# Last image's row-class-0 sums and last column pairs moved from GpSimd to VectorE, and image 0's second normalisation issued four gaps later

## The chip, the cores and the metric

The kernel runs on one core of a Trainium2 chip. The metric is the device time of one execution in microseconds (us), smaller is better. The engines are TensorE (PE, with PEld for its weight loads), VectorE (DVE), ScalarE (ACT), GpSimd (POOL) and SyncE (SP), which issues nearly all DMAs.

## The reference

For two images of 32 channels and 48x48 pixels the kernel computes a cross-scale attention block and then a two-dimensional cosine transform:

```python
x = x + _L0_conv_ref(_gn(x), W1, b1, a1, W2, b2, a2, Wa, ba, aa, Wd, bd)
x = x + _L1_conv_ref(_gn(x))
# _L0_conv_ref, the part that matters here, one image at a time
yi = jnp.einsum('blc,bqc->blq', wn, xp)          # 576 keys x 2304 queries
yi = jax.nn.softmax(yi * SOFTMAX_SCALE, axis=1)  # over the keys
yt = jax.vmap(tconv)(yi, raw_w)                  # stride-2 transposed conv, 6x6 patches
yd = lax.conv_general_dilated(yt, Wd, (2, 2), ((1, 1), (1, 1)), ...)
return (yd + bd) / 6.0
# _L1_conv_ref: y = Dh @ x @ Dw.T per channel, Dh and Dw cosine matrices
```

`_gn` is a group normalisation with one channel per group. The second one (on `x1`, the result of the first line) is the "normalisation" of the title.

## The kernel before, in words

**Queries, keys and classes.** An image's 2304 queries lie in six row classes of 384 (`NCH` = 6), each class in three column tiles of 128 (`TPC` = 3). So there are 12 chunks (`NG`), numbered k = 0 to 11, image 0 being k = 0 to 5, and 36 softmax tiles (`NT`). Each softmax tile is a slot of `nt`, 128 queries by 24x24 keys kept with a zero column (25 per row).

**Attention as sums.** The two convolutions after the softmax are turned into sums of shifted tiles. GpSimd first adds tiles of neighbouring row classes (`total`, lines 667 to 673, called by `row_sums` and, for the classes z5 and z0 that wrap around the image's edge, by `wrapped_sums`). It then adds column tiles in pairs (`pair(k, which)`, lines 647 to 661, two adds per chunk). After that PE transposes and adds (`turn(k, blk)`, line 866, five blocks of keys per chunk, six transposes into one PSUM bank), DVE or ACT copies the bank to `yf` (`sums_copied`, line 1346 on DVE for blocks 0, 2 and 4, line 1084 on ACT for blocks 1 and 3), and PE multiplies with the turned filters (`values(k, blk)`, line 882, five accumulating matmuls per chunk). DVE adds the result to the image (`finish`, line 1361).

**Step numbers.** Everything is issued in an order written out by hand: a loop over 47 steps s on each engine. Chunk k is turned in the steps 11 + 3k to 13 + 3k (j = 0, 1, 2 inside the chunk), so k = 8 has s = 35 to 37, k = 9 has s = 38 to 40, k = 10 has s = 41 to 43 and k = 11 has s = 44 to 46. Each engine executes its instructions in this order, so an instruction that waits holds all that is written behind it. The last three chunks ("flush", `NG - LAG` on) use an order in which a block is copied shortly before its `values`.

**Side jobs.** Work beside the main loop is placed in gaps, three per step. The table `SPREAD` gives each job its first gap and its pace; DVE's and ACT's part comes one or two gaps behind PE's by `BEHIND_PE`. The jobs that matter here belong to the second half of image 0: `x1n` (three DVE instructions, line 1390, `xd` from `v2`, first gap 109 = step 36, gap 1), `zn` (16 transposes of 32 columns three times on PE, line 892, copied out by ACT, line 1094), `d1` (eight cosine matmuls twice, line 902) and `d2` (three long matmuls twice, line 913). `x1n` needs the inverse root of the variance that GpSimd computes in `deviation` (line 614), which stands behind six row sums and three pairs in GpSimd's own order.

**Waits inside turn.** Block m = 5k + blk of `turn` waits until an earlier bank is copied: `wait_copied(m - 2)` up to m = 48 (`FLUSH` is 46), `wait_copied(m - 4)` from 49 on. For m = 47, the block (k = 9, blk = 2), this is the DVE copy of (9, 0). Block 0 of a chunk also waits for the two column pairs of its chunk (`s_pair`).

Of the kernel before, what the change touches and what calls it, by code (L numbers as in the profile page):

```python
# [8 lines left out]
ALU = mybir.AluOpType  # L9
# [3 lines left out]
B, C, H, W = 2, 32, 48, 48  # L13
CR = C // 2
Q = H * W
HL, WL = H // 2, W // 2
# [13 lines left out]
TPC = 3  # L30
JW = W // TPC
NT = B * NCH * TPC
NG = B * NCH
# [7 lines left out]
KP = WL + 1  # L41
PT = (HL + 2) * KP + 2
KROWS = 5
KB = 5
# [3 lines left out]
TURNED = ["z1", "z2", "z3", "z4", "z5", "z0"]  # L48

P0, P1, P2, P3, P4, P5, PAIR0 = 0, 3, 6, 9, 12, 15, (18, 21)  # L50
DOWN0, UP5 = 24, 27
COLS = 30
# [45 lines left out]
    ("norm", 1, 1, 25, 1), ("inorm", 1, 2, 43, 3), ("keys", 1, 2, 46, 3),  # L98
    ("wst", 1, 1, 50, 1), ("bias_a", 1, 1, 53, 1), ("residual", 0, 1, 33, 1),
    ("emb", 1, 2, 57, 3), ("ek", 1, 2, 80, 2), ("residual", 1, 1, 66, 1),  # L100
    ("stats", 0, 6, 98, 1), ("deviation", 0, 1, 105, 1), ("x1n", 0, 3, 109, 2), ("zn", 0, 3, 115, 1),
    ("d1", 0, 2, 122, 2), ("d2", 0, 2, 128, 2)]
CLASSES = [2, 3, 4, 5, 0, 1]


# [28 lines left out]
def sums_done(b, name, jb):  # L134

    return NSUMS * b + SUMS[name] + SUMS_EVERY[name] * jb + 1


def program(nc, x, params, dct, x1_copy, out):
# [16 lines left out]
    with ExitStack() as ctx:  # L156
# [6 lines left out]
        def sem(name):  # L163
            return ctx.enter_context(nc.semaphore(name))

        def sems(name, n=B):
            return [sem(f"{name}{i}") for i in range(n)]
# [31 lines left out]
        nt = sb("nt", [128, NTILES, PT])  # L199
# [35 lines left out]
        zn = sb("zn", [W, C, H])  # L235
# [50 lines left out]
        s_up5 = sems("row_before_shifted_in", TPC)  # L286
# [22 lines left out]
        s_add = sem("row_sums")  # L309
        s_zt = sem("sums_turned")  # L310
        s_pair = sem("columns_paired")
        s_ya = sem("sums_copied_act")
        s_yd = sem("sums_copied_dve")
        s_mb = sem("taps_block_done")
# [54 lines left out]
        def perform(jobs, handlers):  # L369

            for name, b, i in jobs:
                if name in handlers:
                    handlers[name](b, i)
# [44 lines left out]
        def place_of(k):  # L418

            b, i = k // NCH, k % NCH  # L420
            return ((P0, 0), (P1, -1), (P2, -1), (P3, -1), (P4, -1), (PAIR0[b], 0))[i]

        def wait_copied(eng, m):

# [141 lines left out]
        def _(pool):  # L566
# [13 lines left out]
            for blk, row in ((0, 0), (BLOCKS - 1, ROWS - 1)):  # L580
                at = match_rows_at(1, blk, row)
                link(pool.memset(F(strided(mimg[:, :], at, (TILE, TPC), (1, JW))), 0.0))
            link(pool.memset(F(strided(mimg[32:64, :], match_rows_at(0, 0, 0), (BLOCK, BLOCKS), (JW, ROWS))), 0.0))
            at = match_rows_at(TPC + 1, 0, 0) + JW - 1
# [62 lines left out]
            def pair(k, which):  # L647

                if k >= 2:
                    pool.wait_ge(s_zt, KB * (k - 1))  # L650
                place, dr = place_of(k)
                at = (dr + 1) * KP + 1
                dst = nt[:, COLS + 2 * (k % 2) + which, :]
                if which == 0:
                    ins = pool.tensor_tensor(dst[:, at - 1:at + KP * HL], nt[:, place, at - 1:at + KP * HL],  # L655
                                             nt[:, place + 1, at:at + KP * HL + 1], ALU.add)
                else:
                    ins = pool.tensor_tensor(dst[:, at:at + KP * HL], nt[:, place + 2, at:at + KP * HL],  # L658
                                             nt[:, place + 1, at - 1:at + KP * HL - 1], ALU.add)
                ins.then_inc(s_pair, 1)  # L660
                pool.wait_ge(s_pair, 2 * k + which + 1)

            def odd_taps(b, _):
# [4 lines left out]
            def total(b, name, jb, dst, to, one, row1, other, row2, rows):  # L668

                n = KP * rows - 1  # L670
                pool.tensor_tensor(nt[:, dst, (to + 1) * KP + 1:(to + 1) * KP + 1 + n],  # L671
                                   nt[:, one, (row1 + 1) * KP + 1:(row1 + 1) * KP + 1 + n],
                                   nt[:, other, (row2 + 1) * KP + 1:(row2 + 1) * KP + 1 + n],
                                   ALU.add).then_inc(s_add, 1)
                pool.wait_ge(s_add, sums_done(b, name, jb))
                if name in TURNED and jb:
                    pair(NCH * b + TURNED.index(name), jb - 1)

            def wrapped_sums(b, jb):

                for n in (2 * jb, 2 * jb + 1):
                    name, at = ("z5", "z0")[n // TPC], n % TPC
                    if name == "z5":
                        total(b, "z5", at, P4 + at, -1, P4 + at, -1, DOWN0 + at, 1, HL)
                    else:
                        pool.wait_ge(s_up5[at], 16 * (b + 1))
                        total(b, "z0", at, PAIR0[b] + at, 0, PAIR0[b] + at, 0, UP5 + at, -1, HL)
# [46 lines left out]
        def _(pe):  # L734
# [114 lines left out]
            def turn(k, blk):  # L849

                b = k // NCH
                n, r = KEYS[blk], KROWS * blk
                m = KB * k + blk
                if blk == 0:
                    pe.wait_ge(s_pair, 2 * (k + 1))
                if m >= FLUSH + 3:
                    wait_copied(pe, m - 4)
                elif m >= 2:
                    wait_copied(pe, m - 2)
                if m < 2 or FLUSH < m < FLUSH + 3:  # L860
                    pe.wait_ge(s_ex, FILL if m < 2 else NT)
                place, dr = place_of(k)
                first, second = COLS + 2 * (k % 2), COLS + 2 * (k % 2) + 1
                work = ((first, 0, 0), (first, 1, -1), (second, 2, 0), (place + 2, 1, 1), (place + 2, 3, -1), (place, -1, 1))
                for at, (tile, column, shift) in enumerate(work):
                    last = nc.tensor.matmul(turned(sums_bank(m), n, column), keys_at(tile, r + dr, n, shift),  # L866
                                            ident[:, :], start=at == 0, stop=at == len(work) - 1, is_transpose=True,
                                            skip_group_check=True)
                last.then_inc(s_zt, 1)
# [52 lines left out]
            for s in range(steps):  # L922
                k, j = divmod(s - BEGIN, TPC)
# [213 lines left out]
        def _(dve):  # L1137
# [200 lines left out]
            def sums_copied(k, blk):  # L1338
# [5 lines left out]
                else:  # L1344
                    dve.wait_ge(s_mf, misc_no["norm", B - 1, 0] + 1)
                nc.vector.tensor_copy(strided(yf[0:n, blk, :], 0, (1, TPC), (W, ROWS), (TPC, JW)),  # L1346
                                      planes(sums_bank(m), n)).then_inc(s_yd, 1)

            def finish(k, si):

                b, t = k // NCH, ZT[k % NCH]
                if si == 0:
                    dve.wait_ge(s_mb, KB * (k + 1))
                    if k % NCH == 0:
                        dve.wait_ge(s_xres[b], 1)
                        dve.wait_ge(s_apart[b], 1)
                rows = ROWS - 1 if si and t == NCH - 1 else ROWS
                both = v2[2 * C * b:2 * C * (b + 1), :]
                image = strided(both, W * (t + si), (W * NCH, rows), (1, W))
                tap = strided(yt[2 * C * si:2 * C * (si + 1), k % 2, :], 0, (W, rows), (1, W))  # L1360
                nc.vector.scalar_tensor_tensor(out=image, in0=tap, scalar=1.0 / 6.0, in1=image, op0=ALU.mult,  # L1361
                                               op1=ALU.add).then_inc(s_fin, 1)
                dve.wait_ge(s_fin, 2 * k + si + 1)

            def join_taps(b, part):

                first, n = ((2, 4), (0, 2))[part]
                dims = (W * NCH, ROWS), (W, n), (1, W - 1)
                even = strided(x1(b), W * first + 1, *dims)
                odd = strided(v2[2 * C * b + C:2 * C * (b + 1), :], W * first, *dims)  # L1370
                nc.vector.tensor_tensor(even, even, odd, ALU.add).then_inc(s_x1[b], 1)  # L1371
                dve.wait_ge(s_x1[b], part + 1)
# [55 lines left out]
            for s in range(steps):  # L1428
                k, j = divmod(s - BEGIN, TPC)
                if s + 1 == FILL:  # L1430
                    inverse_sum(s)
                if s + 1 < NT:
                    maximum(s + 1)
                if s + 1 < FILL:
                    inverse_sum(s)
                perform(gaps["dve"].get((s, 0), []), handlers)
                if k >= 1 and j == 1:
                    finish(k - 1, 0)
                if k >= 1 and j == 2:
                    finish(k - 1, 1)  # L1440
                if FILL <= s + 1 < NT:
                    inverse_sum(s + 1)
                if k >= 0 and j == 0:
                    sums_copied(k, 0)
                perform(gaps["dve"].get((s, 1), []), handlers)
                if k >= 0 and j == 1:
                    sums_copied(k, 2)
                if k >= 0 and j == 2:
                    sums_copied(k, 4)
                    if k and (k - 1) % NCH >= NCH - 2:  # L1450
                        join_taps((k - 1) // NCH, (k - 1) % NCH - (NCH - 2))
                perform(gaps["dve"].get((s, 2), []), handlers)
            perform(behind[:4], handlers)
            finish(NG - 1, 0)
# [37 lines left out]
```

## Time and profile before

| | us |
|---|---|
| median of 3 runs | 246.06 |
| lowest and highest | 244.96, 249.21 |
| the profiled execution, device time | 246.48 |
| its span, first to last instruction | 244.1 |

| engine | busy us | share of the span |
|---|---|---|
| PE | 178.3 | 73% |
| DVE | 144.3 | 59% |
| POOL | 132.2 | 54% |
| ACT | 116.6 | 48% |

The profiled execution lies 0.42 us above the median. Its device time is 2.4 us more than its span; what lies around the span is the same for both kernels. The mean granted clock of PE is 0.869 of full speed. In the profile a block `turn` is a row "PE L866 ... x6", a block `values` a row "PE L882 ... x2" (each product is recorded as two matmuls).

### The profile page before, as it was taken

Reading aid. Unit: us, or ns where it says so; the run is one execution under the profiler, and the core shown is the slowest. Engines: PE = TensorE matmul, PEld = TensorE weight load, DVE = VectorE, ACT = ScalarE, POOL = GpSimd, SP = SyncE. Lnnn points to the kernel's source line nnn. Section 1 sums busy time; section 2 is a strip of 40 time slices with the busy share of each in tenths; the row PEclk is TensorE's granted clock in tenths of the full one; section 3 lists DMA queues with packets and bytes.
Section 4 is the critical chain, followed back from the end, with each engine's and each line's share of the span. In section 5 each row is a group of like instructions: output and inputs, shape, how many; then the busy total and the mean of one; then the engine's idle time right before and its main releaser. Section 6 shows DMA issues by size and latency. Waiting matters only on the chain. (4 is left out here: it accounts for less than half of the span.)

```text
span 244.1 us, 3460 instructions
## 1 busy us (share of the span) xinstructions
PE 178.3 (73%) x1088; PEld 143.9 (59%) x1088; DVE 144.3 (59%) x291; ACT 116.6 (48%) x211; POOL 132.2 (54%) x114
## 2 busy tenths in 40 slices
PE   0586508576673799751999999969986799992484
PEld 0424507574453577641888878857874587870482
DVE  5678825354224766999465545575793733649502
ACT  4876322575736796632365876536552040220110
POOL 8273001033758999496419499999989586000000
PEclk9996556979795899996799999999999799999555
DMA  5350266551260000244633214400261000000522
GB/s 147 76 96 2 45 123 103 132 125 45 45 103 6 3 0 0 42 82 80 172 99 84 56 32 73 81 8 0 60 137 48 0 4 0 3 0 0 112 37 48
DMA packets 16872, 14.09 MB, mean 58 GB/s; under 512 B 9974, under 2 KB 14646, under 8 KB 16726
## 3 DMA queue, kind: packets, MB, share of 16 engines
q1 hardware_dynamic: 15974, 12.98, 26.5%
q10 hardware_dynamic: 880, 0.89, 1.2%
q8 instruction: 9, 0.15, 0.2%
q14 instruction: 9, 0.07, 0.1%
HBM read 2.14 MB, written 1.18 MB: 14 GB/s over the span
## 5 line engine op out<-in xcount | busy, mean ns | idle before, releaser
L671 POOL TENSOR_TENSOR nt<-nt 128x599 f32<-128x599 f32 (+1 forms) x54 | 73.4, 1360 | 32.6 <-ACT nt L1074 23.5
L882 PE MATMUL yt<-yf,kf 125*128 125x384 f32 (+1 forms) x120 | 50.3, 504 | 6.1 <-DVE yf L1346 4.2
L866 PEld LDWEIGHTS zt<-ident,nt 128*125 128x125 f32 (+1 forms) x312 | 41.6, 180 | 12.9 <-issue 3.5
L866 PE MATMUL zt<-ident,nt 128*125 128x128 f32 (+1 forms) x312 | 43.9, 278 | 0.0
L1066 ACT ACTIVATE nt<-ps,negm 128x576 f32<-128x576 f32 x31 | 22.9, 739 | 39.6 <-DVE negm L1329 39.5
L845 PE MATMUL ps<-wh,vh 128*128 128x288 f32 x62 | 17.8, 371 | 26.9 <-DVE wr L1325 17.0
L1074 ACT ACTIVATE nt<-nt,rps 128x599 f32<-128x599 f32 x36 | 28.6, 796 | 15.4 <-DVE rps L1336 15.2
L1329 DVE TENSOR_REDUCE negm<-ps 128x1 f32<-128x576 f32 x31 | 23.3, 753 | 15.8 <-PE ps L845 15.5
L845 PEld LDWEIGHTS ps<-wh,vh 128*128 128x128 f32 x62 | 10.3, 206 | 32.2 <-DVE wr L1325 17.7
L655 POOL TENSOR_TENSOR nt<-nt 128x601 f32<-128x601 f32 x12 | 16.5, 1371 | 15.3 <-PE zt L866 14.7
L882 PEld LDWEIGHTS yt<-yf,kf 125*128 125x128 f32 (+1 forms) x120 | 19.4, 197 | 8.3 <-DVE yf L1346 4.6
L1346 DVE COPY yf<-zt 125x384 f32<-125x384 f32 (+1 forms) x31 | 21.4, 692 | 4.6 <-issue 4.1
L1084 ACT ACTIVATE yf<-zt 125x384 f32<-125x384 f32 x21 | 14.3, 681 | 10.4 <-PE zt L866 10.4
L658 POOL TENSOR_TENSOR nt<-nt 128x600 f32<-128x600 f32 x12 | 17.7, 1477 | 0.9
L1276 DVE TENSOR_TENSOR mimg<-mst,mhi 96x288 fp32r<-96x288 f32 x16 | 10.6, 664 | 10.7 <-DMA vl<-mimg 5.4
L1336 DVE RECIPROCAL rps<-psm 128x1 f32<-128x1 f32 x36 | 5.8, 160 | 14.8 <-ACT nt L1066 14.6
L1361 DVE SCALAR_TENSOR_TENSOR v<-yt,v 64x384 f32<-64x384 f32 (+1 forms) x24 | 13.2, 548 | 1.8 <-PE yt L882 1.3
L845 PE MATMUL ps<-wl,vh 128*128 128x288 f32 x62 | 14.2, 313 | 0.0
L845 PE MATMUL ps<-wh,vl 128*128 128x288 f32 x62 | 14.2, 313 | 0.0
L845 PE MATMUL ps<-wr,vr 128*128 128x288 f32 x62 | 14.0, 309 | 0.0
L1094 ACT ACTIVATE zn<-pm 48x512 f32<-48x512 f32 x6 | 3.4, 588 | 21.9 <-PE pm L892 21.9
L614 POOL TENSOR_TENSOR mv<-mv,mhalf 32x1 f32<-32x1 f32 x2 | 1.1, 540 | 21.9 <-DVE mv L1149 21.8
(160 smaller groups left out, 319.3 us busy)
## 6 DMA issues: line engine op xcount, KB each, us to landing
nt<-nt SPq DMA_DIRECT2D x12, 285.2 KB, 3.5
vh<-mimg SPq DMA_DIRECT2D x24, 72.0 KB, 2.6
vl<-mimg SPq DMA_DIRECT2D x24, 72.0 KB, 2.5
emb<-emq SPq DMA_DIRECT2D x32, 18.8 KB, 1.8
v<-x SPq DMA_DIRECT2D x2, 288.0 KB, 4.0
vh<-mimg SPq DMA_DIRECT2D x12, 48.0 KB, 2.2
vl<-mimg SPq DMA_DIRECT2D x12, 48.0 KB, 2.2
x_copy<-v SPq DMA_DIRECT2D x2, 288.0 KB, 2.8
```

The costliest lines, as they stand in the source:

```text
L655: ins = pool.tensor_tensor(dst[:, at - 1:at + KP * HL], nt[:, place, at - 1:at + KP * HL], nt[:, place + 1, at:at + KP * HL + 1], ALU.add)
L658: ins = pool.tensor_tensor(dst[:, at:at + KP * HL], nt[:, place + 2, at:at + KP * HL], nt[:, place + 1, at - 1:at + KP * HL - 1], ALU.add)
L671: pool.tensor_tensor(nt[:, dst, (to + 1) * KP + 1:(to + 1) * KP + 1 + n], nt[:, one, (row1 + 1) * KP + 1:(row1 + 1) * KP + 1 + n], nt[:, o ...
L845: last = nc.tensor.matmul(scores_of(t)[:, h, 0:HALF], queries(m, i, jb), w[b][:, HALF * h:HALF * (h + 1)], start=n == 0, stop=n == 3)
L866: last = nc.tensor.matmul(turned(sums_bank(m), n, column), keys_at(tile, r + dr, n, shift), ident[:, :], start=at == 0, stop=at == len(wor ...
L882: nc.tensor.matmul(yt[:, k % 2, 0:CHUNK], kf[b][0:n, blk, :], yf[0:n, blk, :], start=blk == 0, stop=blk == KB - 1).then_inc(s_mb, 1)
L1066: nc.scalar.activation(strided(nt[:, tile_of(g, jb), :], KP + 1, (KP * HL // 2, 2), (KP, HL // 2), (1, WL)), strided(scores_of(t)[:, 0, :] ...
L1074: nc.scalar.activation(tile, tile, ACT.Copy, scale=rps[:, k:k + 1]).then_inc(s_pn, 1)
L1084: nc.scalar.activation(strided(yf[0:n, blk, :], 0, (1, TPC), (W, ROWS), (TPC, JW)), planes(sums_bank(m), n), ACT.Copy).then_inc(s_ya, 1)
L1329: nc.vector.tensor_reduce(negm[:, t % 2:t % 2 + 1], scores_of(t)[:, :, 0:HALF], AX.XY, ALU.max, negate=True).then_inc(s_mx, 1)
L1346: nc.vector.tensor_copy(strided(yf[0:n, blk, :], 0, (1, TPC), (W, ROWS), (TPC, JW)), planes(sums_bank(m), n)).then_inc(s_yd, 1)
L1361: nc.vector.scalar_tensor_tensor(out=image, in0=tap, scalar=1.0 / 6.0, in1=image, op0=ALU.mult, op1=ALU.add).then_inc(s_fin, 1)
```

## The change

The three sums of row class 0 of the last image (`z0`, b = 1) and the two column pairs of the chunks 10 and 11 are issued by DVE instead of GpSimd. The sums come behind the copy of (8, 4), in step 37; the pairs of chunk 10 behind the copy of (9, 4), in step 40; those of chunk 11 behind the copy of (10, 4), in step 43. PE's `turn(10, 0)` and `turn(11, 0)` wait for DVE's pairs. In `SPREAD` the jobs `x1n`, `zn`, `d1` and `d2` of image 0 start four gaps later.

```diff
-    ("stats", 0, 6, 98, 1), ("deviation", 0, 1, 105, 1), ("x1n", 0, 3, 109, 2), ("zn", 0, 3, 115, 1),
-    ("d1", 0, 2, 122, 2), ("d2", 0, 2, 128, 2)]
+    ("stats", 0, 6, 98, 1), ("deviation", 0, 1, 105, 1), ("x1n", 0, 3, 113, 2), ("zn", 0, 3, 119, 1),
+    ("d1", 0, 2, 126, 2), ("d2", 0, 2, 132, 2)]
...
+        def add_pair(eng, k, which):
+            place, dr = place_of(k)
+            at = (dr + 1) * KP + 1
+            dst = nt[:, COLS + 2 * (k % 2) + which, :]
+            if which == 0:
+                return eng.tensor_tensor(dst[:, at - 1:at + KP * HL], nt[:, place, at - 1:at + KP * HL],
+                                         nt[:, place + 1, at:at + KP * HL + 1], ALU.add)
+            return eng.tensor_tensor(dst[:, at:at + KP * HL], nt[:, place + 2, at:at + KP * HL],
+                                     nt[:, place + 1, at - 1:at + KP * HL - 1], ALU.add)
...
-                if name in TURNED and jb:
+                if name in TURNED and jb and (b < B - 1 or name != "z5"):
                     pair(NCH * b + TURNED.index(name), jb - 1)
...
                     name, at = ("z5", "z0")[n // TPC], n % TPC
+                    if b == B - 1 and name == "z0":
+                        continue
...
                 if blk == 0:
-                    pe.wait_ge(s_pair, 2 * (k + 1))
+                    if k < NG - 2:
+                        pe.wait_ge(s_pair, 2 * (k + 1))
+                    else:
+                        pe.wait_ge(s_other, 2 * (k - NG + 3))
...
+            def last_sums():
+                b, g = B - 1, NG - 1
+                for at in range(TPC):
+                    if at == 0:
+                        dve.wait_ge(s_add, sums_done(b, "z4", TPC - 1))
+                    dve.wait_ge(s_up5[at], 16 * B)
+                    n = KP * HL - 1
+                    dst = nt[:, PAIR0[b] + at, KP + 1:KP + 1 + n]
+                    nc.vector.tensor_tensor(dst, dst, nt[:, UP5 + at, 1:1 + n], ALU.add).then_inc(s_last, 1)
+
+            def last_pair(k):
+                dve.wait_ge(s_zt, KB * (k - 1))
+                if k == NG - 2:
+                    dve.wait_ge(s_add, sums_done(B - 1, "z5", TPC - 1))
+                else:
+                    dve.wait_ge(s_last, TPC)
+                for which in range(2):
+                    add_pair(nc.vector, k, which).then_inc(s_other, 1)
...
                     if k and (k - 1) % NCH >= NCH - 2:
                         join_taps((k - 1) // NCH, (k - 1) % NCH - (NCH - 2))
+                if k == NG - 4 and j == 2:
+                    last_sums()
+                if k >= NG - 3 and j == 2 and k < NG - 1:
+                    last_pair(k + 1)
                 perform(gaps["dve"].get((s, 2), []), handlers)
```

**DVE's order from step 35 to step 39.** Before; COPY yf is a bank's copy, SCALAR_TENSOR_TENSOR v is `finish`, TENSOR_SCALAR xd is `x1n`:

```order
L1346 COPY yf<-zt 125x3x128
L1361 SCALAR_TENSOR_TENSOR v<-yt,v 64x8x48
L1390 TENSOR_SCALAR xd<-v,mv 32x768
L1346 COPY yf<-zt 125x3x128
L1390 TENSOR_SCALAR xd<-v,mv 32x768
L1361 SCALAR_TENSOR_TENSOR v<-yt,v 64x8x48
L1346 COPY yf<-zt 100x3x128
L1390 TENSOR_SCALAR xd<-v,mv 32x768
L1346 COPY yf<-zt 125x3x128
```

And in the changed kernel, where TENSOR_TENSOR nt are the three sums:

```order
L1355 COPY yf<-zt 125x3x128
L1391 SCALAR_TENSOR_TENSOR v<-yt,v 64x8x48
L1355 COPY yf<-zt 125x3x128
L1391 SCALAR_TENSOR_TENSOR v<-yt,v 64x8x48
L1355 COPY yf<-zt 100x3x128
L1367 TENSOR_TENSOR nt<-nt 128x599 x3
L1420 TENSOR_SCALAR xd<-v,mv 32x768
L1355 COPY yf<-zt 125x3x128
L1420 TENSOR_SCALAR xd<-v,mv 32x768 x2
```

The copies in these rows are those of the blocks (8, 0), (8, 2), (8, 4) and (9, 0). `x1n` no longer stands ahead of the copies of (8, 2) and (8, 4); three sums and one `x1n` now stand ahead of the copy of (9, 0).

**DVE's order around the pairs of chunk 10**, from the copy of (9, 4), the changed kernel:

```order
L1355 COPY yf<-zt 100x3x128
L431 TENSOR_TENSOR nt<-nt 128x601
L433 TENSOR_TENSOR nt<-nt 128x600
L1355 COPY yf<-ps 125x3x128
L1391 SCALAR_TENSOR_TENSOR v<-yt,v 64x8x48
```

The two adds stand between the copies of (9, 4) and (10, 0), where nothing stood before; the same pair of rows stands between the copies of (10, 4) and (11, 0).

**PE's order from `turn(9, 4)` to `turn(10, 1)`.** Before, with one half of `d1` (L902) in it:

```order
L866 MATMUL zt<-ident,nt 100x8x16 x6
L902 MATMUL pm<-cosm,zn 96x48 x8
L882 MATMUL yt<-yf,kf 128x384
L866 MATMUL ps<-ident,nt 125x8x16 x6
L882 MATMUL yt<-yf,kf 128x384
L866 MATMUL ps<-ident,nt 125x8x16 x6
```

In the changed kernel:

```order
L875 MATMUL zt<-ident,nt 100x8x16 x6
L891 MATMUL yt<-yf,kf 128x384
L875 MATMUL ps<-ident,nt 125x8x16 x6
L891 MATMUL yt<-yf,kf 128x384
L875 MATMUL ps<-ident,nt 125x8x16 x6
```

Only `values(9, 2)` is left between `turn(9, 4)` and `turn(10, 0)`. Both halves of `d1` now come after `turn(10, 2)`; between `turn(10, 4)` and `turn(11, 0)` stand `values(10, 2)` and one half of `d2`, and the other half of `d2` stands behind `turn(11, 2)`.

## Rows read from the trace of the kernel before

**Rows 1.** The page, part 1: engine, busy us (share), instructions.

```profile
PE 178.3 (73%) x1088; PEld 143.9 (59%) x1088; DVE 144.3 (59%) x291; ACT 116.6 (48%) x211; POOL 132.2 (54%) x114
```

**Rows 2.** The chain that ended last: start, us, what.

```profile
190.50 1.65 PE yt L882 x2
...
210.17 1.05 PE pm L913 x6
...
219.14 0.67 DVE yf L1346
```

**Rows 3.** The waits from 183 to 222 us: total, times, longest.

```profile
PE yt L882 <- DVE yf L1346: 4.2, 2, 3.5
...
DVE xd L1390 <- POOL mv L614: 3.9, 1, 3.9
```

**Rows 4.** The timeline of DVE: start, us, what, [idle before <- releaser].

```profile
188.22 1.64 DVE L1390 TENSOR_SCALAR xd<-v,mv 32x768 f32<-32x768 f32 x1 [3.86 <-POOL mv L614]
189.78 0.66 DVE L1346 COPY yf<-zt 125x384 f32<-125x384 f32 x1
```

**Rows 5.** Busy time by stage; behind the engines PE's granted clock, DMA.

```profile
187.00:190.50 3.50, 0.04 (x2) 0.01 (x1) 2.29 (x3) 0.68 (x1) 3.26 (x4) 1.00 0.00 0
190.50:194.00 3.50, 3.50 (x10) 2.44 (x11) 1.91 (x3) 0.00 (x0) 0.89 (x2) 0.52 0.00 0
194.00:221.00 27.00, 26.99 (x210) 20.90 (x208) 13.73 (x22) 6.61 (x11) 10.77 (x8) 1.00 0.01 2
```

**Rows 6.** The timeline of PE: turn (8,3), (10,0), (11,0), (11,2).

```profile
186.22 0.82 PE L866 MATMUL zt<-ident,nt 128*125 128x128 f32 x6
...
203.76 0.82 PE L866 MATMUL ps<-ident,nt 128*125 128x128 f32 x6
...
213.01 0.82 PE L866 MATMUL ps<-ident,nt 128*125 128x128 f32 x6
...
215.62 0.82 PE L866 MATMUL zt<-ident,nt 128*125 128x128 f32 x6
```

**Rows 7.** DVE's copy of (11,2), behind the last row above.

```profile
216.53 0.67 DVE L1346 COPY yf<-zt 125x384 f32<-125x384 f32 x1 [0.16 <-PE zt L866]
```

**Rows 8.** The timeline of POOL: sums of z5; second pair of chunk 10.

```profile
188.20 2.76 POOL L671 TENSOR_TENSOR nt<-nt 128x599 f32<-128x599 f32 x2
...
196.41 1.45 POOL L658 TENSOR_TENSOR nt<-nt 128x600 f32<-128x600 f32 x1
```

**Rows 9.** The timeline of DVE while POOL is idle.

```profile
219.85 1.72 DVE L1371 TENSOR_TENSOR v<-v 32x1504 f32<-32x1504 f32 x1
...
225.13 0.94 DVE L1371 TENSOR_TENSOR v<-v 32x752 f32<-32x752 f32 x1
...
228.48 1.85 DVE L1390 TENSOR_SCALAR xd<-v,mv 32x768 f32<-32x768 f32 x3 [0.72 <-POOL mv L614]
```

**Rows 10.** DVE adds of 288 columns: POOL idle, then POOL busy.

```profile
34.71 0.46 DVE L1323 TENSOR_TENSOR wl<-wim,wh 128x288 fp32r<-128x288 f32 x1 [4.76 <-ACT wr L1057]
...
104.17 1.28 DVE L1323 TENSOR_TENSOR wl<-wim,wh 128x288 fp32r<-128x288 f32 x1
105.49 1.42 DVE L1324 TENSOR_TENSOR wr<-wim,wr 32x288 fp32r<-32x288 f32 x1
```

**Rows 11.** POOL adds of 624 columns: DVE idle, then beside Rows 10.

```profile
51.41 1.29 POOL L671 TENSOR_TENSOR nt<-nt 128x624 f32<-128x624 f32 x1 [12.56 <-ACT nt L1074]
...
102.30 5.91 POOL L671 TENSOR_TENSOR nt<-nt 128x624 f32<-128x624 f32 x4 [3.28 <-ACT nt L1074]
```

**Rows 12.** Stages of PE alone: us, PE busy, granted clock, DMA.

```profile
107.40:111.00 3.60, 0.00 (x0) 1.00 0.67 107
111.00:114.70 3.70, 0.00 (x0) 0.63 0.38 65
...
118.00:119.00 1.00, 1.00 (x4) 0.60 0.16 43
```

**Rows 13.** The page, part 5: ACT's copies of zn.

```profile
L1094 ACT ACTIVATE zn<-pm 48x512 f32<-48x512 f32 x6 | 3.4, 588 | 21.9 <-PE pm L892 21.9
```

More of the change, by code:

```diff
@@ L311, in program @@
         s_pair = sem("columns_paired")
+        s_last = sem("last_row_sums")
+        s_other = sem("last_columns_paired")
         s_ya = sem("sums_copied_act")
@@ L650, in pair @@
                     pool.wait_ge(s_zt, KB * (k - 1))
[L651 to L660, printed above, removed]
+                add_pair(nc.gpsimd, k, which).then_inc(s_pair, 1)
                 pool.wait_ge(s_pair, 2 * k + which + 1)
```

## The prediction, made before the changed kernel ran

> **What bounds the kernel now.** I read the page first: PE is busy 73% of the span, DVE 59%, GpSimd 54% [rows 1]. No engine is full, so I followed the chain that ended last. It runs on PE alone from 190.50 us, block after block, until DVE's copy of the last turned block at 219.14 [rows 2]; the rest of the span, 25 us, is a chain on DVE, then PE, that both kernels share. So the change is worth what it does to the moment at which `turn(11, 4)` is done.
>
> Then I read the waits. In this stretch PE has one long wait, 3.46 us before `values(8, 2)`, for a DVE copy, and DVE has one of 3.86 us, before the first `x1n`, for GpSimd's inverse root [rows 3, 4]. They are one wait. `x1n` stands ahead of the copy of (8, 2); DVE can start it at 188.22, GpSimd's next add holds it for about 1 us, and the copy follows at 189.78. PE's granted clock, which was 1.00 during the wait, is 0.52 from 190.5 to 194, that is the lower level, 1.2 GHz instead of 2.4, for nearly all of it [rows 5]. In those 3.5 us PE did the work of 1.8, so the clock cost another 1.7. Together the stall is worth 3.5 + 1.7 = 5.2 us. Behind it PE is busy 26.99 of 27.00 us at full clock [rows 5]: there every new wait of PE adds its full length.
>
> **Edit 1, `x1n` and what follows it four gaps later.** It removes the 5.2 us: the copy of (8, 2) then waits for its turned block only. `zn`, `d1` and `d2` are the same instructions as before. No DMA moves: SP's order is unchanged, and ACT only gets its copies later. But moving PE's side jobs takes away cover, which I price below. The three groups of transposes of `zn` now stand together. The third needs the bank that ACT empties after the first, and ACT has the copy of (9, 3), 0.68, ahead of its own 0.59 [rows 13]: 0.2 + 0.7 + 0.6 = 1.5 us against 1.2 of PE's work on two groups. **Wait added: 0.3 us.**
>
> **Edit 2, seven adds leave GpSimd.** GpSimd had the pairs of chunk 10 ready at 197.9 and PE took them at 203.76 [rows 6, 8]; those of chunk 11 were as early against 213.01. GpSimd is 6 us ahead, so taking 7 x 1.4 us from it gains nothing. The Trainium skill (GPSIMD Engine Reference, Engine selection) would have a two-input elementwise add on VectorE, with GpSimd about half as fast, which speaks for the move; the rows say that the adds are shorter but not that anyone waits for them. What it would be if someone did is the last case below.
>
> **Edit 3, the same seven adds on DVE.** DVE has no add of 600 columns in this trace. Its nearest ones, with GpSimd idle, are 1504 columns in 1.72 us and 752 in 0.94 [rows 9], so 1.04 ns per column and 0.16 fixed: 0.78 us for 600. The upper end for one is GpSimd's own time, 1.45 [rows 8]. What matters is where they stand.
>
> *The three sums* stand ahead of the copy of (9, 0), and `turn(9, 2)` waits for that copy. Without the old stall PE is through `turn(8, 3)` at 186.9. A block takes 0.65 us, so six more blocks (`values(8, 2)` to `turn(9, 1)`) bring it to **190.8**. DVE copies (8, 4) when `turn(8, 4)` is done, 188.2 + 0.2 (the delay that [rows 6, 7] show, 216.28 to 216.53) + 0.68, so it is free at 189.1. With GpSimd idle the three sums would end at 191.4, `x1n` (1.85 / 3 = 0.62 [rows 9]) at 192.0, the copy at 192.7. But GpSimd is not idle: it does the sums of z5 from 188.20 on [rows 8], now three in a row to about 192.3 by themselves.
>
> What happens when both add shows at 104 us. DVE's add of 288 columns, 0.46 alone, took 1.28 and 1.42 while GpSimd ran back to back [rows 10], and GpSimd's four took 5.91 with their gaps instead of 4 x 1.29 + 0.2 = 5.4 [rows 11]. That looks like taking turns: each DVE add waits for the end of GpSimd's add, then GpSimd waits for DVE's.
>
> Taking turns: GpSimd's first sum ends at 189.5, DVE's first streams 0.6 to 190.1, GpSimd's second 1.25 to 191.4, DVE's second to 192.0, GpSimd's third to 193.3, DVE's third to 194.0. Then `x1n` 194.6, copy of (9, 0) 195.3. **PE waits from 190.8 to 195.3, 4.5 us.** The bounds are 1.9 us (no interference; 192.7) and this 4.5. I take the upper one, since the rows nearest to it, at 104 us, show a turn of GpSimd before every DVE add.
>
> *The pairs of chunk 10* stand behind the copy of (9, 4). After `turn(9, 4)` DVE needs 0.2 + 0.68 + 2 x 0.78 = 2.45 us, GpSimd being idle by then. PE has `values(9, 2)`, 0.65, before `turn(10, 0)`: the half of `d1` that stood there, 1.5 us, has moved away. **Wait added: 1.8 us.**
>
> *The pairs of chunk 11* likewise: 2.45 us, covered by `values(10, 2)`, 0.65, and half of `d2`, 1.05 / 2 = 0.5 [rows 2]. **Wait added: 1.3 us.**
>
> Behind DVE's adds its later instructions slip too (copies, `finish`), but PE waits for the pairs first, so they are in these numbers. The tail is unchanged: DVE's copy of (11, 4) still follows `turn(11, 4)`.
>
> **The sum.** New waits 4.5 + 0.3 + 1.8 + 1.3 = 7.9 us; removed 3.5 of wait and 1.7 of slow clock. That is +2.7 if PE's clock stays at full speed, and +4.4 if the new 4.5 us wait costs the 1.7 again. Against the profiled execution's 246.48 these are **249.2** and **250.9**. It lies 0.4 above the median of 246.06, less than the runs scatter (244.96 to 249.21), so I don't correct for it. Does the clock fall? The old wait of 3.46 us ended just as it fell; in the long idle time from 107.4 it was still 1.00 up to 111.0 and averaged 0.63 over the next 3.7 us, so it fell after about 4.6 us [rows 5, 12]. A wait of 4.5 lies between: nearly even, slightly for staying.
>
> **The cases.** 2% of 246.06 is 4.9 us, about what a measurement of this kernel can tell from no change: faster is below 241.1, slower above 251.0.
>
> - *Turns, clock stays*: 249.2. Chance 0.33. Forecast.
> - *Turns, clock falls*: 250.9. Chance 0.25, of which a third lies above 251.0.
> - *DVE keeps its turn.* The three sums have no wait between them once the first has run, while at 104 us each DVE instruction waited for the one before. If DVE's second and third add come before GpSimd gets back, the sums end at 191.5, but `x1n` meets GpSimd's second sum and ends at 193.2, copy at 193.9. PE's wait is 3.2 instead of 4.5: 247.9. Chance 0.20.
> - *No interference.* The wait is 1.9: new waits 5.3 against 5.2 removed: 246.6. Against it stand the 1.28 and 1.42. Chance 0.10.
> - *The clock stays low for longer.* After the idle time at 107.4 PE ran at half speed from 114.7 to about 118.8, and the clock had been low since about 112, some 6.8 us in all [rows 12], twice as long as at 190.5. If the clock falls in PE's wait at 195 and PE works 6.9 us at half speed instead of 3.5, that costs 1.7 more: 252.6, slower by 2.7%. It decides from a wait in which the clock falls and that is followed by a further wait, and the 1.8 us wait at `turn(10, 0)` comes soon after. For it: PE's next blocks are broken by that wait. Against it: dense blocks ended the low clock after 3.5 us at 190.5. Chance 0.07.
> - *The shorter adds count.* If PE's pace in the last chunks hangs on the seven adds, each is 1.4 - 0.8 = 0.6 us shorter on DVE, 4.2 us in all: 246.48 - 4.2 = 242.3, and lower if the 5.2 us go as well. This is the Trainium skill's preference taken at its word. The 6 us by which the pairs are early speak against it. Chance 0.05, half of it over 2% faster.
>
> So the likeliest is 249.2, slower by 1.3% but within 2%. Slower than 251.0: 0.07 + a third of 0.25, 0.15. Faster: 0.03. Within: 0.82. The range 246.0 to 251.3 leaves out the last two cases and the edges of two others, about 0.2.
>
> **What the profile after would show.** The 3.86 us wait of DVE for the root is gone and PE runs without a gap to about 190.8. Then PE waits before `turn(9, 2)` for DVE's copy of (9, 0), 4.5 us if the engines take turns (DVE's sums 1.1 to 1.9 us each, GpSimd's second and third sum 1.9 instead of 1.25), 3.2 if DVE's come in a row, 1.9 if there is no interference (0.78 each). Two waits for DVE's pairs, 1.8 and 1.3 us, precede `turn(10, 0)` and `turn(11, 0)`. DVE's copy of (11, 4) starts at 221.9 with a full clock (219.14 before). The prediction is wrong if the sums find GpSimd done, if DVE's adds of 600 columns take much more or less than 0.8, or if the clock behaves otherwise.

## The result and the profile after

The changed kernel takes **253.75 us** (median of 4 runs, 252.78 to 255.46) against 245.51 (median of 4, 244.75 to 249.21): ratio 1.035, 95% interval 1.028 to 1.043. It is slower by 8.2 us. The prediction said 249.2, slower by 1.3% and within 2%, with a range up to 251.3. The direction was right, the size was not. The ratios and intervals here and below leave out executions over 1.5% slower than the fastest of their kernel, which the medians include, and three executions that profiles were taken of (e1, e2, e4) are among those left out, since PE's clock was lower in them ahead of the part that is compared.

I compare the two profiled executions (255.46 and 246.48 us) by one **stretch**: from the start of `values(7, 4)`, the last PE block before the changed part, to DVE's copy of (11, 4), from which on both chains are alike. Before, it runs from 182.86 to 219.14, 36.3 us; after, from 184.52 to 228.70, 44.2 us, which is **+7.9**. The rest is 25.0 us behind it in both, 1.7 us ahead of it, where nothing was changed (see the last section), and 0.6 us less around the span (1.8 instead of 2.4).

The timeline of PE in the changed kernel, from `turn(9, 1)` to `turn(10, 2)`, and `turn(11, 0)`. It answers to [rows 2, 6]:

```profile
191.79 0.82 PE L875 MATMUL ps<-ident,nt 128*125 128x128 f32 x6
196.47 1.64 PE L875 MATMUL ps<-ident,nt 128*125 128x128 f32 x6 [3.86 <-DVE yf L1355]
197.91 1.48 PE L891 MATMUL yt<-yf,kf 125*128 125x384 f32 x2
199.19 1.49 PE L875 MATMUL zt<-ident,nt 128*125 128x128 f32 x6
200.60 2.93 PE L901 MATMUL pm<-ident,xd 32*48 32x32 f32 x48
203.46 1.65 PE L891 MATMUL yt<-yf,kf 125*128 125x384 f32 x2
204.90 1.49 PE L875 MATMUL zt<-ident,nt 128*100 128x128 f32 x6
206.18 1.49 PE L891 MATMUL yt<-yf,kf 125*128 125x384 f32 x2
208.72 1.64 PE L875 MATMUL ps<-ident,nt 128*125 128x128 f32 x6 [1.05 <-DVE nt L433]
210.15 1.49 PE L891 MATMUL yt<-yf,kf 125*128 125x384 f32 x2
211.43 1.14 PE L875 MATMUL ps<-ident,nt 128*125 128x128 f32 x6
212.41 0.81 PE L891 MATMUL yt<-yf,kf 100*128 100x384 f32 x2
...
221.95 0.92 PE L875 MATMUL ps<-ident,nt 128*125 128x128 f32 x6 [0.93 <-DVE nt L433]
```

The brackets are the three new waits: 3.86 us for the copy of (9, 0) and 1.05 and 0.93 for DVE's pairs. The second column is what the prediction missed. From 196.47 to about 212 a block takes 1.3 us from start to start instead of 0.65. The stages of PE alone (us, PE busy, granted clock, DMA), the answer to [rows 5]:

```profile
187.00:192.40 5.40, 5.40 (x36) 1.00 0.00 0
192.40:196.40 4.00, 0.21 (x2) 0.83 0.00 0
196.40:212.00 15.60, 14.47 (x83) 0.50 0.01 2
212.00:230.00 18.00, 17.07 (x112) 1.00 0.00 1
```

The clock fell inside the wait, at about 195.0 (0.83 is the mean of full and half speed over the 4.0 us), when PE had been idle for 2.4 us. It stayed at its lower level, 1.2 GHz, for the next 15.6 us, in which PE was busy 14.47. Half of that, 7.2 us, is lost work by the granted clock, against the 1.7 before. The waits come to 3.9 + 1.1 + 0.9 = 5.8 against 3.5. So about +5.5 of clock and +2.4 of waits, 7.9 us in all.

DVE and GpSimd at the place of the first wait (two timelines):

```profile
190.09 0.69 DVE L1355 COPY yf<-zt 100x384 f32<-100x384 f32 x1 [1.33 <-issue]
190.82 4.44 DVE L1367 TENSOR_TENSOR nt<-nt 128x599 f32<-128x599 f32 x3
195.18 0.66 DVE L1420 TENSOR_SCALAR xd<-v,mv 32x768 f32<-32x768 f32 x1
195.77 0.64 DVE L1355 COPY yf<-zt 125x384 f32<-125x384 f32 x1
```

```profile
189.88 4.73 POOL L675 TENSOR_TENSOR nt<-nt 128x599 f32<-128x599 f32 x3
```

DVE's three sums took 4.44 us, GpSimd's three beside them 4.73. The old stall of DVE [rows 4] is gone, and the copy of (9, 0) is now what comes late.

### The profile page after: what moved, and what is told of

It reads as the page before. It is cut to its first block and busy times, and to the rows that moved or that the text cites. A ratio compares the mean times of both kernels' runs of the same rounds, so it can differ in the third digit from the quotient of the medians.

```text
span 253.7 us, 3456 instructions
## 1 busy us (share of the span) xinstructions
PE 187.7 (74%) x1088; PEld 151.8 (60%) x1088; DVE 149.6 (59%) x298; ACT 116.9 (46%) x211; POOL 123.0 (48%) x107
## 5 line engine op out<-in xcount | busy, mean ns | idle before, releaser
L675 POOL TENSOR_TENSOR nt<-nt 128x599 f32<-128x599 f32 (+1 forms) x51 | 69.5, 1362 | 32.6 <-ACT nt L1083 22.5
L891 PE MATMUL yt<-yf,kf 125*128 125x384 f32 (+1 forms) x120 | 52.9, 527 | 1.6 <-ACT yf L1093 0.9
L875 PEld LDWEIGHTS zt<-ident,nt 128*125 128x125 f32 (+1 forms) x312 | 44.4, 191 | 13.8 <-issue 4.7
L875 PE MATMUL zt<-ident,nt 128*125 128x128 f32 (+1 forms) x312 | 46.3, 289 | 0.0
L851 PE MATMUL ps<-wh,vh 128*128 128x288 f32 x62 | 18.8, 389 | 26.0 <-DVE wr L1334 16.1
L891 PEld LDWEIGHTS yt<-yf,kf 125*128 125x128 f32 (+1 forms) x120 | 20.2, 204 | 3.5 <-ACT yf L1093 1.1
L431 POOL TENSOR_TENSOR nt<-nt 128x601 f32<-128x601 f32 x10 | 14.1, 1405 | 14.3 <-PE zt L875 13.8
L1285 DVE TENSOR_TENSOR mimg<-mst,mhi 96x288 fp32r<-96x288 f32 x16 | 9.7, 605 | 11.9 <-DMA vl<-mimg 6.6
L433 POOL TENSOR_TENSOR nt<-nt 128x600 f32<-128x600 f32 x10 | 14.9, 1490 | 0.8
L875 PEld LDWEIGHTS ps<-ident,nt 128*125 128x125 f32 (+1 forms) x48 | 7.7, 218 | 9.3 <-DVE yf L1355 4.0
```

Source lines behind the costliest of these rows:

```text
L431: return eng.tensor_tensor(dst[:, at - 1:at + KP * HL], nt[:, place, at - 1:at + KP * HL], nt[:, place + 1, at:at + KP * HL + 1], ALU.add)
L433: return eng.tensor_tensor(dst[:, at:at + KP * HL], nt[:, place + 2, at:at + KP * HL], nt[:, place + 1, at - 1:at + KP * HL - 1], ALU.add)
L851: last = nc.tensor.matmul(scores_of(t)[:, h, 0:HALF], queries(m, i, jb), w[b][:, HALF * h:HALF * (h + 1)], start=n == 0, stop=n == 3)
L891: nc.tensor.matmul(yt[:, k % 2, 0:CHUNK], kf[b][0:n, blk, :], yf[0:n, blk, :], start=blk == 0, stop=blk == KB - 1).then_inc(s_mb, 1)
```

## The experiments

All kernels were timed beside the kernel before on one chip; its median there was 246.35 (e1 to e4) and 246.36 (e5 to e8). "Stretch" is the one defined above, from each run's profile: 36.3 before, 44.2 with the full change.

**e1: the table alone.** The kernel before with only the change of `SPREAD`, the first four changed lines of the diff.

> Only the table is changed (image 0's second normalisation and what follows it four gaps later); all seven adds stay on GpSimd. Theory A, the clock theory: the loss of the full change comes from PE's 3.9 us wait for the copy of (9,0), after which PE worked 14.6 us at half speed (7.3 us lost). Without adds on DVE there is no such wait and no low clock between 187 and 229, so this is faster than before by the whole removed stall, 3.5 + 1.7 = 5.2 us less 0.3: 240.5 to 241.5. Theory B, the transposes theory: the 48 transposes of 32 columns of zn, now in one group, take the clock down or keep it down by themselves: then the low clock stays, some 5 to 7 us, and the time is 244 to 248.

Measured: 243.78 us (241.03 to 244.81), ratio 0.987, interval 0.980 to 0.995. Stretch 31.6 (186.00 to 217.61), **-4.7**; PE's granted clock was full in all of it. The stage of PE, and PE's only long bracket there:

```profile
186.00:217.60 31.60, 30.81 (x237) 1.00 0.04 11
```

```profile
197.96 0.62 PE L892 MATMUL pm<-ident,xd 32*48 32x32 f32 x16 [0.79 <-ACT zn L1094]
```

So the table does nearly what the prediction said (-5.2 + 0.3), though the new wait is 0.8 us and not 0.3, and grouping the small transposes did not take the clock down in this run. The median moved less than the stretch and lies above the 240.5 to 241.5 of theory A; it is the stretch and its clock that speak for A. This profile's stretch began 3.1 us later than the one of before.

**e2: the adds alone.** The full change with the old table (those four lines reversed).

> Only the seven adds move to DVE, the table is that of before. Both theories: the old stall of 3.5 us stays. DVE's three sums come when GpSimd has nearly finished the sums of z5, so about 2.3 us for three; they delay the copy of (9,0) by that, and turn(9,2) by about 1 us. turn(10,0) waits about 0.3 us (half of d1 stands before it), turn(11,0) about 1.8. Theory A: PE's waits after the old stall are short, so the clock comes back after about 3.5 us as before and the kernel is 3 us slower than before, 248 to 249. Theory C, that the adds on DVE cost what the whole change costs, whatever the table: 253 to 254.

Measured: 248.63 us (247.21 to 252.65), ratio 1.012 (1.007 to 1.016). Stretch 39.7 (186.23 to 225.89), **+3.4**. Theory C falls. The old stall is still there. DVE's sums stand further back and don't meet GpSimd's, whose three ended at 195.88:

```profile
197.59 2.17 DVE L1367 TENSOR_TENSOR nt<-nt 128x599 f32<-128x599 f32 x3
```

```profile
191.59 4.29 POOL L675 TENSOR_TENSOR nt<-nt 128x599 f32<-128x599 f32 x3
```

2.17 us for three, less than half of 4.44. The adds cost one longer wait, and the clock was low for longer than the 3.5 us that theory A expected, though only whole `turn` and `values` blocks stood behind the stall:

```profile
219.65 0.92 PE L875 MATMUL ps<-ident,nt 128*125 128x128 f32 x6 [1.45 <-DVE nt L433]
```

```profile
193.80:200.40 6.60, 6.53 (x19) 0.52 0.00 0
```

That is 3.2 us of lost speed instead of 1.7, so nearly half of the +3.4 is clock. Why it came back later than in the kernel before is open. The two edits together cost 7.9 us, but one by one -4.7 and +3.4: the loss is in their meeting.

**e3: no clash of the two engines.** The full change, and in `wrapped_sums`:

```diff
+                if b == B - 1 and jb == 0:
+                    pool.wait_ge(s_last, TPC)
```

> The full change, but GpSimd's three sums of z5 for the last image wait until DVE's three sums of z0 are done, so the two engines never add at the same time there. DVE's three should take 2.2 us instead of 4.44. PE's wait before turn(9,2) goes from 3.9 to about 1.7 us. Theory A: a wait of 1.7 us leaves the clock at full speed, so both 2.2 us of wait and 7.3 us of slow clock go: 244 to 245. Theory B: only the 2.2 go: 251 to 252.

Measured: 247.45 us (245.88 to 249.25), ratio 1.006 (1.003 to 1.010). Stretch 36.5 (184.45 to 220.97), **7.7 us less than the full change**. DVE's sums and `x1n`, GpSimd's sums, and PE's waits:

```profile
190.74 2.17 DVE L1369 TENSOR_TENSOR nt<-nt 128x599 f32<-128x599 f32 x3
```

```profile
193.05 4.58 POOL L675 TENSOR_TENSOR nt<-nt 128x599 f32<-128x599 f32 x3 [3.30 <-DVE nt L1369]
```

```profile
194.11 0.92 PE L877 MATMUL ps<-ident,nt 128*125 128x128 f32 x6 [1.57 <-DVE yf L1357]
198.17 0.62 PE L903 MATMUL pm<-ident,xd 32*48 32x32 f32 x16 [0.79 <-ACT zn L1105]
202.62 0.92 PE L877 MATMUL ps<-ident,nt 128*125 128x128 f32 x6 [1.68 <-DVE nt L433]
214.21 0.92 PE L877 MATMUL ps<-ident,nt 128*125 128x128 f32 x6 [0.93 <-DVE nt L433]
```

```profile
187.00:222.00 35.00, 30.03 (x227) 1.00 0.00 1
```

The clock is 1.00 over the whole stretch. Without the clash the first wait is 2.3 us shorter, and with it the slow clock is gone. The same blocks, from `turn(9, 2)` to the end of `turn(10, 1)`, took 8.1 us here and 14.9 in the full change, waits left out, so the slow clock cost 6.8 us, a little less than half of the busy time. Of the 2.3 + 6.8 us 1.4 come back: at full speed PE gets to ACT's copy and to the pairs earlier and waits 0.8 and 0.6 us more. This pair of profiles is the fairest comparison: the stretch began at 184.45 here and at 184.52 in the full change, with the same granted clock ahead of it (0.74 from 60 to 100 us, 0.87 to 140, 0.96 to 182). I had expected 244 to 245 and had left these 1.4 us out, so the time missed by 2.5 us.

**e4: the wait filled.** The full change, and before `turn(9, 2)` on PE 33 transposes of the identity into a free bank. Their result is not used.

```diff
+FILLER = 33
...
+                if k == NG - 3 and j == 0:
+                    for r in range(FILLER):
+                        nc.tensor.matmul(pm[:, 0, 0:128], ident[:, :], ident[:, :], start=True, stop=True,
+                                         is_transpose=True, skip_group_check=True)
```

> The full change, and in the wait before turn(9,2) PE does 33 transposes of 128 columns of the identity into a free PSUM bank that nobody reads, 3.6 us of work in a wait of 4.0. Nothing else moves: the wait for the copy of (9,0) is as long as in the full change, only PE isn't idle in it. Theory A: the clock stays at full speed, 7.3 us less than the full change: 246 to 247. Theory B: the clock still falls at zn: 252 to 254.

Measured: 250.54 us (247.09 to 252.51), ratio 1.010 (1.001 to 1.020). Stretch 39.5 (186.16 to 225.67), 4.7 us less than the full change, though DVE's sums took 4.45 us again and the copy was no earlier:

```profile
192.45 4.45 DVE L1372 TENSOR_TENSOR nt<-nt 128x599 f32<-128x599 f32 x3
```

```profile
194.09 3.77 PE L952 MATMUL pm<-ident 128*128 128x128 f32 x33
198.11 0.92 PE L876 MATMUL ps<-ident,nt 128*125 128x128 f32 x6 [0.26 <-DVE yf L1360]
```

```profile
198.00:203.00 5.00, 4.09 (x63) 1.00 0.01 2
203.40:206.90 3.50, 2.87 (x9) 0.51 0.00 0
```

The same lateness with a busy PE costs 4.7 us less: the idle time had taken the clock down. But here it fell once later, at 203.4, just behind the small transposes with their 0.8 us wait, and cost 1.4. With it 250.5 us lies between the 246 to 247 of theory A and the 252 to 254 of theory B. Theory A is right on the first fall. The second stands where theory B puts one, but the same transposes and the same wait brought none in e1 and e3, so what brought it here is not shown.

**e5: the full change again**, unaltered.

> The full change again, unaltered, beside the others on one chip, since the time of one execution also hangs on where PE's clock falls before 183 us (8.3 us of lost PE work in one profile, 14.3 in another). Clock theory: the stretch from values(7,4) to DVE's copy of (11,4), 44.2 us in the first profile, is 41 to 45 again, with PE's wait of about 3.9 us before turn(9,2), and the low clock behind it lasts 7 to 17 us. Rival: that profile was a mishap of the clock and the stretch comes out at 38 to 40; the median is then about 248.

Measured: 254.53 us (252.71 to 255.86), ratio 1.034 (1.028 to 1.041). Stretch 44.4 (182.59 to 226.99), first wait 3.87, and the clock low from 193.5 to 210.6. It was no mishap.

**e6: the small transposes later.** The full change with another table:

```diff
-    ("stats", 0, 6, 98, 1), ("deviation", 0, 1, 105, 1), ("x1n", 0, 3, 113, 2), ("zn", 0, 3, 119, 1),
-    ("d1", 0, 2, 126, 2), ("d2", 0, 2, 132, 2)]
+    ("stats", 0, 6, 98, 1), ("deviation", 0, 1, 105, 1), ("x1n", 0, 3, 113, 2), ("zn", 0, 3, 127, 1),
+    ("d1", 0, 2, 132, 1), ("d2", 0, 2, 136, 1)]
```

> The full change, but zn, d1 and d2 of image 0 stand still later: PE has six long blocks (7.8 us at half speed) behind its 3.9 us wait before anything else, instead of three and then the 48 small transposes. If it is the small transposes and the wait behind them that keep the clock low for 17 us, the low clock now ends 3.5 to 7 us after PE resumes, the stretch from values(7,4) to DVE's copy of (11,4) is about 4 us shorter than the full change's 44.2, and the time is 249 to 250. If the length of the wait alone sets how long the clock stays low, nothing changes: 253 to 254.

Measured: 248.76 us (248.17 to 251.37), ratio 1.013 (1.006 to 1.019). Stretch 39.8 (184.83 to 224.61), 4.4 us less than the full change, with a first wait of 3.83 us, as long as there. The stages of PE:

```profile
196.70:202.00 5.30, 5.24 (x16) 0.50 0.02 3
202.00:224.00 22.00, 20.12 (x170) 1.00 0.00 1
```

The clock fell as before but was full again 5.3 us after PE resumed, behind four dense blocks; 2.7 us were lost instead of 7.2. So the wait makes the clock fall, and what PE does behind it helps to set for how long. It is not the only thing: with whole blocks behind the wait the low clock lasted 3.5 us in the kernel before, 5.3 here and about 6.3 in e2.

**e7: only the pairs on DVE.** The full change, with `last_sums` left out and GpSimd doing z0's sums again, for which the pairs of chunk 11 then wait; the main lines are

```diff
-                    if b == B - 1 and name == "z0":
-                        continue
...
-                if k == NG - 4 and j == 2:
-                    last_sums()
```

> The full change with the three sums of z0 back on GpSimd; only the four column-pair adds are on DVE. No wait before turn(9,2). PE waits about 1.7 us before turn(10,0) and about 1 us before turn(11,0), no fall of the clock: the stretch from values(7,4) to DVE's copy of (11,4) is 2.5 us longer than with all adds on GpSimd (31.6 in that profile), 34.2, and the time 245 to 247, so no gain over the table alone. If the clock also falls on these two short waits, as much as 3 us more.

Measured: 246.09 us (244.13 to 249.94), ratio 1.000 (0.996 to 1.003). Stretch 35.9 (183.16 to 219.01), 4.2 more than e1, with the clock at 1.00 throughout. The waits are 1.68 and 0.92 us for the pairs and, not expected, 0.89 before `turn(9, 2)`, where `x1n` met GpSimd. Moving the pairs eats what the table gains, with no help from the clock.

**e8: the table, and PE kept busy at the end.** The table of e1 with all adds on GpSimd, `zn` with pace 2 instead of 1, and behind the last `values` 66 transposes of the identity whose result is not used:

```diff
+TAIL = 66
...
             values(NG - 1, 4)
+            wait_emptied(pe, "d2", 0, 1)
+            for r in range(TAIL):
+                nc.tensor.matmul(bank(misc_no["d2", 0, 1])[:, 0:128], ident[:, :], ident[:, :], start=True, stop=True,
+                                 is_transpose=True, skip_group_check=True)
             perform(behind, handlers)
```

> All adds on GpSimd and the later gaps, zn spread so that its third group does not wait for ACT (0.8 us less), and 66 transposes of the identity (7.2 us) behind PE's last values, where PE idles 8 us while DVE does the last statistics, at the end of which the clock is at half speed. Clock theory: the last 10.7 us of PE work then run at full speed, so up to 5 us less: 237 to 239. Rival: the last part is bound by latencies between ACT, DVE and PE, or its small matmuls bring the clock down at once, and the gain is below 1.5 us: 242 to 243.

Measured: **239.66 us** (237.71 to 243.78), ratio 0.971, interval 0.965 to 0.977: faster than both kernels, by 2.9% than the one before. Stretch 31.0 (182.74 to 213.74), 0.6 less than in e1, and behind it 22.7 us instead of the 25.0 of before and of e1. The stages of PE at the end, and below them the one of the kernel before:

```profile
215.40:223.00 7.60, 7.39 (x67) 1.00 0.18 40
223.80:228.30 4.50, 3.53 (x68) 1.00 0.74 128
228.30:233.00 4.70, 4.58 (x21) 0.50 0.04 7
```

```profile
229.00:244.00 15.00, 10.66 (x86) 0.50 0.34 60
```

The clock is full at the start of this work, where it was 0.50 before, but falls again at 228.3 among the small matmuls, so 2.3 of the up to 5 us that I expected come.

## Why the prediction was wrong

**The bound.** Right: PE's chain, and the removed stall with its slow clock. e1 gives -4.7 for the -4.9 forecast, with a wait of 0.8 us for `zn` where 0.3 was added.

**GpSimd off the path.** Right: the adds moved away gained nothing (e2, e7).

**DVE's adds.** Right: 0.79 and 0.78 us alone at `turn(10, 0)` (forecast 0.78), and taking turns beside GpSimd, 4.44 us for three (forecast 4.9), where e3 shows 2.17 without. The case "DVE keeps its turn" is out.

**PE's waits.** Forecast 4.5, 0.3, 1.8 and 1.3, 7.9 in all; measured 3.86, 0, 1.05 and 0.93, 5.8. The first came out shorter mainly because three turns took 4.44 us and not 4.9. At half speed PE is later at the pairs and at ACT's copy; at full speed e3 shows 0.79, 1.68 and 0.93 for the last three. This term was 2.1 us too large.

**The clock.** This is the step that failed: "that is +2.7 if PE's clock stays at full speed, and +4.4 if the new 4.5 us wait costs the 1.7 again." I took over the price of the fall at 190.5, where PE went on with dense blocks, as a constant. It was 7.2 us by the granted clock, 6.8 by the comparison with e3. The forecast case had no fall at all, so the clock term was 7.2 us short and the waits 2.1 too large, which is 5.1 of the 5.2 us by which the stretch missed (+7.9 for +2.7). The choice of that case was wrong by its own rows too. The old wait of 3.46 us had "ended just as it fell", so a wait of 4.5 was more likely than not to bring the fall, and the measured one of 3.86 did, 2.4 us after PE's last block; the 4.6 us of idleness at 107.4 [rows 12] was no guide to it. I had seen that the low clock at 112 lasted twice as long [rows 12], and priced that in a rival at only one more 1.7 us and a chance of 0.07. That rival had the right mechanism, a fall in this wait and a further wait soon after, and it was on the side where the result came out; its 252.6 is 1.2 short of the median. It came that near with 3.4 us for the clock, 3.8 too little, and waits 2.1 too long, so the nearness is partly luck.

**What stays open.** e6 moved the transposes away from the first wait, and that ended the low clock early; whether the transposes or the 1.05 us wait at 207.7 held it down longer was not separated. Nor do I know in how many executions of the kernel before the clock falls in the old 3.46 us wait; its profile is one of them, and that of e2, with the same wait, another. All stretches come from one execution of each kernel, two of the full change.

## What to carry to other kernels

Price a wait of TensorE by what it does behind the wait too: here 3.9 us of idleness cost 3.9 us plus about 7 of slow clock, or plus 2.7 with dense matmuls behind it. Don't give work of an engine that is early to one whose queue others wait in, and least of all at a moment when both add from SBUF, since they then take turns. Where an idle time of TensorE can't be removed, unused matmuls in it can pay: 4.7 us in e4.

## What the runs showed of the hardware

**Two adding engines take turns.** Three DVE adds of 599 columns: 2.17 us alone, 4.42 to 4.45 beside GpSimd's three in four profiles, though none of DVE's waited for the one before by a semaphore. GpSimd's three took 4.73 beside them and 4.29 in e2. The Trainium skill (SBUF — State Buffer, Who interferes with whom) calls the shared port pair an exclusive lock held for a whole instruction; the trace agrees (4.44 us for 2.17 us of adds), and adds that here the lock changed hands after each: GpSimd's adds ended at about 191.1, 192.8 and 194.6 us, DVE's 0.6 to 0.7 us behind each of them.

**The clock can fall while PE works on small matmuls.** In e8 it fell at 228.3, with PE busy 3.53 of the 4.5 us before, on transposes of 32 columns and the cosine products of `d1`; in e4 it fell at 203.4 behind 48 such transposes. It is not always so: in e1, e3 and e7 the same 48 transposes ran at a granted clock of 1.00, and so did all behind them in the stretch.

**The clock varies ahead of the change.** Between 60 and 100 us, where both kernels run the same part of the program, the granted clock was 0.87 in the profile of before and 0.74 in that of after:

```profile
60.00:100.00 40.00, 29.85 (x167) 0.87 0.15 25
```

```profile
60.00:100.00 40.00, 32.22 (x166) 0.74 0.15 25
```

The stretch began between 182.6 and 186.2 us in ten profiles. That moves the time of a profiled execution by up to 3.6 us whatever the change does, and is why the stretch tells more than the time.
